# Attention scores from two fp32r parts, two heads side by side in row tiles of TensorE

## The reference

```
x = x + 0.5 * ffn(layernorm(x))      # 8 experts, each silu(x Wg) * (x Wu), then Wd, F = 256; weights per token from a router
x = x + attn(layernorm(x))           # 16 heads of 16, causal, softmax(q k^T / 4) v, then Wo
x = x + 0.5 * ffn(layernorm(x))
```

## Time and profile before

| | |
|---|---|
| Median of 3 runs | 778.74 us (778.41 to 781.88) |
| Profiled execution, its own time | 779.27 us |
| Its span in the trace | 777.5 us |
| Granted TensorE clock, mean | 0.995 of 2.4 GHz |
| HBM read, written | 67.78 MB, 12.71 MB |

### The profile page before, as it was taken

The page is one execution under the profiler, slowest core; times in us unless marked ns, Lnnn a source line. Parts: engine busy times, 40 slices in busy tenths (PEclk is TensorE's granted clock), DMA queues, the critical chain, the costliest instruction groups (busy, mean ns, idle before and its releaser), DMA issues.

```text
span 777.5 us, 14076 instructions
## 1 busy us (share of the span) xinstructions
PE 758.5 (98%) x4878; PEld 606.8 (78%) x4878; DVE 476.2 (61%) x1316; ACT 348.5 (45%) x657; POOL 417.0 (54%) x497
## 2 busy tenths in 40 slices
PE   6979999999999999999999999999999999999998
PEld 5868878976778777777778778677777778888887
DVE  6847754596657857787556667855657433473333
ACT  4455425525446544656344456453463453423222
POOL 4384867246654444844454853454554655655663
PEclk9999999999999999999999999999999999999999
DMA  9236423363213631323531222433222132223231
GB/s 304 84 103 192 163 74 105 103 201 96 70 55 92 177 101 62 103 62 106 161 117 48 82 86 89 140 97 109 77 89 83 48 104 82 82 67 124 84 117 58
DMA packets 60807, 81.57 MB, mean 105 GB/s; under 512 B 8384, under 2 KB 44608, under 8 KB 60736
## 3 DMA queue, kind: packets, MB, share of 16 engines
q1 hardware_dynamic: 58544, 80.36, 32.5%
q10 hardware_dynamic: 2192, 0.32, 0.2%
HBM read 67.78 MB, written 12.71 MB: 104 GB/s over the span
## 4 chain that ended last, share of the span: by engine, by line
PE 90%; DVE 6%; POOL 1%; issue 1%; DMA 1%; ACT 0%; DVEq 0%; POOLq 0%
PE ra L746 15%; PE ra L747 14%; PE ra L748 14%; PE dn L768 8%; PE dn L769 7%; PE dn L770 7%; PE ra L879 5%; PE ra L867 5%; PE ra L852 5%; PE ra L723 3%; PE ra L820 1%; PE ra L834 1%; PE ra L835 1%; PE ra L836 1%; PE ra L797 1%
## 5 line engine op out<-in xcount | busy, mean ns | idle before, releaser
L1357 POOL TENSOR_TENSOR hid<-hid,wb 128x512 f32<-128x512 f32 x124 | 161.5, 1303 | 183.0 <-DVE hid L1218 176.8
L746 PE MATMUL ra<-xt_hi,wgu_hi 128*128 128x512 f32 x512 | 226.5, 442 | 0.0
L1361 POOL TENSOR_TENSOR ht_lo<-hid,ht_hi 128x512 fp32r<-128x512 f32 x124 | 162.0, 1308 | 120.2 <-ACT ht_hi L997 119.8
L747 PE MATMUL ra<-xt_hi,wgu_lo 128*128 128x512 f32 x512 | 203.1, 397 | 0.0
L748 PE MATMUL ra<-xt_lo,wgu_hi 128*128 128x512 f32 x512 | 202.4, 395 | 0.0
L1269 DVE CUSTOM_DVE_ANT_0 junk<-ra,mask 128x128 bf16<-128x128 f32 (+3 forms) x256 | 121.0, 487 | 84.0 <-PE ra L852 81.3
L768 PE MATMUL dn<-wd,ht_hi 128*128 128x256 f32 x512 | 162.6, 318 | 2.7 <-POOL ht_lo L1361 2.7
L1210 DVE SCALAR_TENSOR_TENSOR hid<-hid,ra 128x512 f32<-128x512 f32 x125 | 85.7, 686 | 125.0 <-ACT hid L989 124.0
L769 PE MATMUL dn<-wd,ht_hi 128*128 128x256 f32 x512 | 144.9, 283 | 0.0
L770 PE MATMUL dn<-wd,ht_lo 128*128 128x256 f32 x512 | 144.5, 282 | 0.0
L997 ACT ACTIVATE ht_hi<-hid 128x512 fp32r<-128x512 f32 x124 | 78.0, 630 | 144.0 <-POOL hid L1357 119.4
(11 more groups left out here) (164 smaller groups left out, 859.4 us busy)
## 6 DMA issues: line engine op xcount, KB each, us to landing
wd<-wd_parts SPq DMA_DIRECT2D x56, 512.0 KB, 3.6
wb<-wts_rows SPq DMA_DIRECT2D x62, 256.0 KB, 3.7
qk_parts<-parts SPq DMA_DIRECT2D x32, 192.0 KB, 2.1
q_st<-qk_parts SPq DMA_DIRECT2D x96, 64.0 KB, 2.2
k_st<-qk_parts SPq DMA_DIRECT2D x96, 64.0 KB, 2.2
wd_parts<-wd SPq DMA_DIRECT2D x8, 512.0 KB, 3.0
x_res<-in_x SPq DMA_DIRECT2D x4, 512.0 KB, 8.5
stage<-in_Wg SPq DMA_DIRECT2D x8, 256.0 KB, 5.3
```

Source lines behind the costliest of these rows:

```text
L746: mm(b_, w_hi, xt_hi[q % 2][:, c, :], start=c == 0, stop=False)
L747: mm(b_, w_lo, xt_hi[q % 2][:, c, :], start=False, stop=False)
L1357: nc.gpsimd.tensor_tensor(tb, tb, wb[m % NWB][:, :], ALU.mult).then_inc(hw_done, 1)
L1361: nc.gpsimd.tensor_tensor(ht_lo[n % NHT][:, :], hidden(n)[:, :], f32(ht_hi[n % NHT][:, :]), ALU.subtract).then_inc(lo_done, 1)
```

## The change

Queries, keys and maxima are split into two fp32r parts, not three bf16 ones; three products of 16 rows make 48 rows, 50 with the maxima's. Two heads lie in the stacks side by side, one on partitions 0 to 63, one on 64 to 127, and their matmuls go to the two halves of the array's rows, one after the other in the order, each into its own bank. The number of score matmuls and their columns stay. Each half has its own semaphore. The third part's ScalarE and VectorE steps are gone; the parts store has 256 KB instead of 192; "mx" has four DMAs instead of two; "st" has twelve as before.

```diff
-Q_PARTS = (0, 0, 0, 1, 1, 2)
-K_PARTS = (0, 1, 2, 0, 1, 0)
+Q_PARTS = (0, 0, 1)
+K_PARTS = (0, 1, 0)
+NTILE = 2
+ROWS = P // NTILE
+TH = GH // NTILE
...
-                put(meet[g] - PERIOD + 0.15 + 0.27 * k if b + g else meet[0] - 2.1 + 0.115 * k, ("max", b, g, k))
+                put(meet[g] - PERIOD + 0.15 + 0.54 * (k // NTILE) if b + g else meet[0] - 2.1 + 0.23 * (k // NTILE),
+                    ("max", b, g, k))
...
-                put(meet[g] + 1.1 + 0.33 * r, ("exp", b, g, r))
+                put(meet[g] + 1.1 + 0.66 * (r // NTILE), ("exp", b, g, r))
...
-                             rank=self.target[item] + FIRST[eng].get(item[0], BEFORE[eng]))
+                             rank=self.target[item] + FIRST[eng].get(item[0], BEFORE[eng]) - sooner)
...
-            width = (0.11, 0.118, 0.175, 0.232)
+            width = (0.07, 0.118, 0.175, 0.232)
...
-                add("pe", ("max", b, g, k), width[k % QT], ("sp", "st", b, g), ("pe", "mt") + ago(2) if G >= 2 else None)
+                t, i = k % NTILE, k // NTILE % QT
+                add("pe", ("max", b, g, k), width[i] if t else 0.03, ("sp", "st", b, g), ("pe", "mt") + ago(2) if G >= 2 else None,
+                    more=0.0 if t else width[i], sooner=1.0 * t)
...
-                add("pe", ("exp", b, g, r), row[r % PB], ("act", "mx", b, g))
+                t, w = r % NTILE, row[r // NTILE]
+                add("pe", ("exp", b, g, r), w if t else 0.03, ("act", "mx", b, g), more=0.0 if t else w, sooner=1.0 * t)
...
-        q_st = sb("q_st", [P, NST, GH, T], BF16)
-        k_st = sb("k_st", [P, NST, GH, T], BF16)
+        q_st = sb("q_st", [P, NST, TH, T], F32R)
+        k_st = sb("k_st", [P, NST, TH, T], F32R)
...
-                        mm(o[:, 0:(i + 1) * P], q_st[0:KROWS, G % NST, hh, i * P:(i + 1) * P],
-                           k_st[0:KROWS, G % NST, hh, 0:(i + 1) * P], start=True, stop=True).then_inc(ra_full, 1)
+                        mm(o[:, 0:(i + 1) * P], q_st[rows, G % NST, h, i * P:(i + 1) * P],
+                           k_st[rows, G % NST, h, 0:(i + 1) * P], start=True, stop=True).then_inc(row_full[t], 1)
...
-                        for hp, j, c in LAYOUT[r % PB]:
-                            hh = 2 * pr + hp
-                            last = mm(o[:, c:c + T - j * P], k_st[0:SROWS, G % NST, hh, j * P:(j + 1) * P],
-                                      q_st[0:SROWS, G % NST, hh, j * P:T], start=True, stop=True)
-                        last.then_inc(ra_full, 1)
+                        for h, j, c in LAYOUT[r // NTILE]:
+                            last = mm(o[:, c:c + T - j * P], k_st[rows, G % NST, h, j * P:(j + 1) * P],
+                                      q_st[rows, G % NST, h, j * P:T], start=True, stop=True)
+                        last.then_inc(row_full[t], 1)
...
-                    if kind == "ql":
-                        b, f, u = it[1:]
-                        k = b * 8 + f * 4 + u
-                        act.wait_ge(*emptied(("qk", b, f, u)))
-                        nc.scalar.activation(parts[k % 2][:, 1, :], rest[:, :], ACT.Copy).then_inc(qk_m, 1)
...
-                        for c in range(2):
-                            act.dma_start(q_st[KROWS + c:KROWS + c + 1, G % NST, :, :].rearrange("a h t -> a (h t)"),
-                                          mp[:, c, :]).then_inc(mx_ld[G % NST], 16)
+                        for t in range(NTILE):
+                            for c in range(2):
+                                row = t * ROWS + KROWS + c
+                                act.dma_start(f32(q_st[row:row + 1, G % NST, :, :]).rearrange("a h t -> a (h t)"),
+                                              f32(mp[TH * QT * t:TH * QT * (t + 1), c, :])).then_inc(mx_ld[G % NST], 16)
...
-                        nc.vector.tensor_tensor(parts[k % 2][:, 2, :], rest[:, :], parts[k % 2][:, 1, :],
-                                                ALU.subtract).then_inc(qk_l, 1)
```

More of the change, by code:

```diff
@@ L224, in __init__, with add @@
         self.target, self.ops, self.next = target, {}, {}
-    def add(self, eng, item, length, *needs, port=False, takes=None, frees=None, holds=None, lets=None, kb=0, more=0.0, then=()):
+    def add(self, eng, item, length, *needs, port=False, takes=None, frees=None, holds=None, lets=None, kb=0, more=0.0, then=(),
+            sooner=0.0):
         key = (eng,) + item
@@ L526, in build @@
         PE_ORDER, ACT_ORDER, DVE_ORDER, POOL_ORDER, SP_ORDER = (order[e] for e in ("pe", "act", "dve", "pool", "sp"))
-        USE = {it: k for k, it in enumerate(it for it in PE_ORDER if it[0] in RING)}
+        USE = {it: k for k, it in enumerate(it for it in PE_ORDER if it[0] in RING and it[0] not in ("max", "exp"))}
+        TILE_USE = {it: k for t in range(NTILE)
+                    for k, it in enumerate(it for it in PE_ORDER if it[0] in ("max", "exp") and it[3] % NTILE == t)}
         MAX_USE = {it: k for k, it in enumerate(it for it in DVE_ORDER if it[0] == "max")}
@@ L602, in build @@
         x2_lo = sb("x2_lo", [P, KT, T], F32R)
-        parts = [sb(f"parts{i}", [P, 3, HT], BF16) for i in range(2)]
-        rest = sb("rest", [P, HT])
+        parts = [sb(f"parts{i}", [P, 2, HT], F32R) for i in range(2)]
         def over(name, shape, dt, at):
@@ L665, in build @@
         ra_full = sem("ra_full")
+        row_full = [sem(f"row_full{t}") for t in range(NTILE)]
         ra_free = [sem(f"ra_free{i}") for i in range(NBANK)]
@@ L918, in _ @@
                         act.wait_ge(consts, CONSTS)
-                        for c in range(2):
-                            act.dma_start(k_st[KROWS + c:KROWS + c + 1, :, :, :].rearrange("a s h t -> a (s h t)"),
-                                          minus[48 * c:48 * (c + 1), :]).then_inc(minus_in, 16)
+                        for c in range(2 * NTILE):
+                            row = c // 2 * ROWS + KROWS + c % 2
+                            act.dma_start(f32(k_st[row:row + 1, :, :, :]).rearrange("a s h t -> a (s h t)"),
+                                          minus[24 * c:24 * (c + 1), :]).then_inc(minus_in, 16)
                     if kind == "bias":
@@ L1037, in _ @@
                         if G >= NST:
-                            act.wait_ge(ra_full, full(("exp", (G - NST) // GR, (G - NST) % GR, GB - 1)))
-                        for c in range(2):
-                            act.dma_start(q_st[KROWS + c:KROWS + c + 1, G % NST, :, :].rearrange("a h t -> a (h t)"),
-                                          mp[:, c, :]).then_inc(mx_ld[G % NST], 16)
+                            for t in range(NTILE):
+                                act.wait_ge(*row_tile(("exp", (G - NST) // GR, (G - NST) % GR, GB - NTILE + t)))
+                        for t in range(NTILE):
+                            for c in range(2):
+                                row = t * ROWS + KROWS + c
+                                act.dma_start(f32(q_st[row:row + 1, G % NST, :, :]).rearrange("a h t -> a (h t)"),
+                                              f32(mp[TH * QT * t:TH * QT * (t + 1), c, :])).then_inc(mx_ld[G % NST], 16)
                     if kind == "exp":
@@ L1046, in _ @@
                             act.wait_ge(ra_full, full(prev))
-                        nc.scalar.activation(probs[:, r // PB, r % PB, :], o[:, :], ACT.Exp,
+                        act.wait_ge(*row_tile(it))
+                        nc.scalar.activation(probs[:, r % NTILE, r // NTILE, :], o[:, :], ACT.Exp,
                                              scale=HD ** -0.5).then_inc(freed, 1)
@@ L1248, in _ @@
                         dve.wait_ge(qk_h, k + 1)
[L1249 to L1257, removed]
-                        nc.vector.tensor_tensor(parts[k % 2][:, 2, :], rest[:, :], parts[k % 2][:, 1, :],
-                                                ALU.subtract).then_inc(qk_l, 1)
+                        nc.vector.scalar_tensor_tensor(out=parts[k % 2][:, 1, :], in0=o[:, 0:HT],
+                                                       scalar=bias[:, u // 2:u // 2 + 1], in1=f32(parts[k % 2][:, 0, :]),
+                                                       op0=ALU.add, op1=ALU.subtract).then_inc(freed, 1)
                     if kind == "max":
                         b, g, s = it[1:]
-                        w = (s % QT + 1) * P
+                        w = (s // NTILE % QT + 1) * P
+                        col = (s % NTILE * TH + s // NTILE // QT) * QT + s // NTILE % QT
                         if b + g + s == 0:
@@ L1362, in _ @@
                                                 ALU.subtract).then_inc(lo_done, 1)
-                    if kind == "exp" and it[3] % PB == PB - 1:
-                        pr = it[3] // PB
+                    if kind == "exp" and it[3] // NTILE == PB - 1:
+                        pr = it[3] % NTILE
                         pool.wait_ge(*emptied(it))
@@ L1431, in _ @@
                         if G >= NST:
```

(13 more changed lines are left out.)

59 lines of the change are left out of this document (30 added, 29 removed).

## The result

The changed kernel takes 822.8 us (median of 4 runs, 820.9 to 823.4), the kernel before 780.1 (778.4 to 781.9): ratio 1.054, 95% interval 1.052 to 1.057, so 43 us slower. The forecast was 811, in a range of 742 to 836.

What follows compares the result with a forecast made beforehand. TensorE was taken as the full engine. From the profiled 779.3 us, 37.9 saved by running pairs side by side and 70 added by 159 excursions at 0.44 gave 811 us, in a range of 742 to 836.

Steps and rivals of the forecast that it cites:

- What bounds it: Whole kernel: TensorE is full, busy for 758.5 of 777.5 us, and the other engines have room.
- row writes of the maxima: On ScalarE's queue: 64 writes instead of 32, priced at nothing; 19 us at most if uncovered.
- Part 1, side by side: Score matmuls: a pair on the array's halves costs one stream, 42.8 us instead of 80.7, saving 37.9.
- That end of the range: Narrow pairs: fp32r at 128 columns streaming like plain fp32, 0.213 us at worst; +6 us kept for the range.
- Part 2, the price of an excursion: Score pairs among FFN matmuls: leaving the whole-array tiling and returning costs 0.44 us, 0.24 in and 0.20 out.
- L879's 0.20: Exit from L879 (probs times V, four column tiles): the next matmul adds 0.43 instead of 0.23, 0.20 us lost.
- L879's 0.16: Entry to L879: the block adds 2.29 us against 2.13 of streaming, 0.16 lost with weights of 32 columns.
- How many excursions: Score steps among FFN work: 208 x 13/17 = 159 excursions, bounds 120 to 208, costing 70 us.
- free borders: At pairs and the FFN matmul behind: weight loads pulled ahead as at the transpose; 744 us, chance 0.22.
- Half a price: At the borders: one border drains, or half-array loads are covered; 32 us of cost, 773 us, chance 0.13.
- Nothing runs together: In row tiles: a pair's matmuls don't overlap; 849 us with borders paid, no change with free borders; chance 0.05.
- The signs: Longer VectorE wait for L852, TensorE at 98%, pair's first some 0.24 above its stream, FFN matmul behind it 0.43.

Runs made afterwards that it cites:

- bf16 parts: Changed kernel with two bf16 parts instead of two fp32r ones, same tiles and order: 798.5 us, ratio 1.023.
- same-half run: Changed kernel with both matmuls of a pair reading the first half's rows, so both run in one row tile: 862.9 us, ratio 1.106.
- packed kernel: Changed kernel with max scores sharing banks (160 pair steps, not 208) and two pair steps due together: 773.3 us, ratio to before 0.992.
- whole-array profiles: Every score matmul on the whole array, adding up two heads' scores: in the changed kernel 786.0 us, in the packed order 785.9 us.
- product run: Changed kernel with the 16 transposes of the maxima done as plain fp32 products with the identity: 826.2 us, one run.
- whole-array run: Changed kernel with every score matmul on the whole array, adding up two heads' scores: 786.0 us, ratio to before 1.008.

## Why the prediction was right

**What bounds it**: as read. TensorE stayed at 98%, and all that moved is in its steps. The row writes of the maxima and the dropped third part show nowhere among its waits.

**Part 1, side by side**: forecast 80.7 - 42.8 = 37.9 us saved. The second pair of an excursion adds 0.24 for two matmuls of 512 columns, that is one stream, and undoing the overlap cost 40 us. By the matmul ends the scores cost 83.0 us before, not 80.7, and after, without the borders, 121.8 - 78 = 43.8, not 42.8: 39.2 us saved. Right. Fp32r at 128 columns was no slower than its weight load: the narrow pair's 0.26 leaves 0.05 to 0.06 after the 0.20 to 0.21 of the way in. That end of the range can go.

**Part 2, the price of an excursion**: 0.44 forecast, 0.39 measured. Coming out was exactly L879's 0.20. Going in was 0.20 and not 0.24: to L879's 0.16 I added 0.08 for wider weights, but the 0.16 already held 0.05 beyond the standing still, which I read as the loads of the narrow tiles and their starts (not tested). The standing still is 0.10 to 0.11 on either kind of tile. Part of the difference is one of reckoning: L879's loss was taken against the pure stream, and by that measure going in is 0.43 - 0.213 = 0.22 here.

**How many excursions**: this is the term that was mis-sized. 13 groups for 17 steps was taken over, 159; there are 200 for 208 pair steps. The ratio of before did hold for before (323 groups for 416 steps), but half as many steps among the same FFN chunks meet half as often: before, 93 of 416 steps joined another's group, after, 26 of 226. These 226 are the 208 steps and the second halves of 18 split pairs, where I had allowed for ten. 200 x 0.39 = 78 against the forecast 70 us.

**Not forecast**: the three clock dips, 5.1 us. 8 of excursions and 5.1 of dips, less the 1.3 by which part 1 saved more, are the 11.8 between forecast and result. That the parts close so well is partly luck: executions of one kernel differ by some 2 us, and the forecast started 0.8 below the median of before.

**The rivals**: free borders (744) rested on the transpose, and the product in its place shows why that row was no witness. Half a price (773) did not occur; even the bf16 parts, whose load shows nowhere, still pay 0.11 + 0.20, some 0.3 per excursion. Nothing runs together (849) is what the same-half run shows, 863.

**The signs** came, but for one size: VectorE's wait for the max scores is 97.7 us instead of 81.3, TensorE is at 98%, the groups are within 120 to 208, a pair adds no more than a lone matmul of its width (0.431 and 0.430 at 512 columns), the FFN matmul behind adds 0.43; the pair's first adds 0.20 to 0.22 above its stream and not 0.24.

## What to carry to other kernels

A row-tiled matmul costs its stream shared among tiles, and, with fp32r weights of 128 columns, about 0.4 us of TensorE for each time the program leaves the whole-array tiling and returns. Count excursions, not matmuls: at 512 columns one pair by itself costs 0.43 + 0.20 = 0.63 us against 0.46 on the whole array, two pairs in one excursion 0.66 + 0.20 = 0.86 against 0.92. So two of the widest pairs are just ahead, and narrower ones are not: with two pair steps per excursion this kernel is still slower than before (793 us). In an order that interleaves small steps with other work, the meeting has to be arranged (due times and free banks), as the packed kernel does. Read the price of a border from any tiled block that is already there, and don't take a transpose for one.

## What the runs showed of the hardware

- **Going in and out are alike**: 0.10 to 0.11 us in which nothing starts after the last stream, then a weight load uncovered: 0.11 for 128 columns of fp32r, none to be seen for bf16. The Trainium skill, TensorEngine Tiling (Array Packing), Key Properties, states that a change of tiling mode drains TensorE; the trace agrees, with these numbers. A transpose with 16 weight columns shows no such cost (0.11 us, nothing late); whether it changes the tiling at all, no run here shows. Behind an excursion transposes pay too: four add 0.59 at 303.94 instead of 0.44.
- **A single tile pays too**: 0.43 for a lone 512-column matmul in a row tile and 0.20 behind it, as for a pair; for the lone product of 16 weight columns 0.10 going in (0.32 less its own 0.22) and 0.20 behind.
- **The clock**: in the changed kernel the granted clock fell to 1.2 GHz three times inside the attention. Ahead of the dip at 166.6 TensorE was idle for 0.7 of 3.4 us, between score matmuls that waited for VectorE's maxima (the first window above). Ahead of the other two it has no idle time by the profile. Ahead of the dip at 357.8 it did this (chain of waits):

```profile
354.78 0.44 PE ra L734 x4
355.21 0.01 PE ra L807
355.23 0.11 PE ra L808
...
357.35 0.43 PE ra L864 x2
357.79 0.46 PE dn L779
```

Four transposes, sixteen router matmuls of 16 columns each that take 0.11 for their weights, and a pair with its standing still; ahead of the dip at 627.4 a lone score matmul and sixteen router matmuls. The kernel before does the router's work too and had no dip in this stage, nor had the whole-array profiles, in the changed order or in the packed one. That the standing still at the borders brings the dips fits these profiles, but it was not tested, and their number doesn't follow the number of excursions: three here, one in the product run with the same 200 and one with the bf16 parts, two with 112, none with 80. Nor does a mean clock of one execution settle it: those of the whole-array run were granted 0.991 to 0.996, and those of the kernel before 0.993 to 0.997.
